# Cross stage: the first tile's first eight heads go to the DMA transpose as well, and all hinges and the gate come ahead of the third query's parts

## The reference

```python
x = x + _L0_attn_ref(_layernorm(x), ...)          # self attention over the batch axis, 16 heads of 32
x = x + _L0_xattn_ref(_layernorm(x), ctx, ctx, mask, ...)
x = x + _L0_ffn_ref(_layernorm(x), ...)

# cross attention
scores = jnp.einsum('bnlh,bnph->bnlp', qm, km) / np.sqrt(HEAD_DIM)
scores = jnp.where(mask, scores, MASK_FILL)
attn = jax.nn.softmax(scores, axis=-1)
out = jnp.einsum('bnlp,bnph->bnlh', attn, vm)
# ffn: 64 small functions of one variable, each a sum over 16 hinges
s = jnp.einsum('btd,dm->btm', x, Win) + bin_
h = jax.nn.relu(s[..., None] * W1 + b1)
g = jnp.einsum('btmh,mh->btm', h, W2) + b2
out = jnp.einsum('btm,md->btd', g, Wout) + bout
```

## Time and profile before

| | us |
|---|---|
| median of 3 runs | 1730.53 (1727.5 to 1731.91) |
| the profiled execution, its own time | 1728.16 |
| its span, first to last instruction | 1726.2 |
| TensorE busy | 1614.0 (93%) |
| VectorE busy | 1401.6 (81%) |
| GpSimd busy | 1172.5 (68%) |
| ScalarE busy | 975.0 (56%) |
| mean granted TensorE clock | 0.979 |

### The profile page before, as it was taken

One profiled execution on the slowest core, in us unless ns is written; L12 is line 12 of the kernel. 1 busy time (PEld: TensorE's weight loads), 2 busy tenths in 40 slices (PEclk: granted clock), 3 DMA queues, 4 the chain that ended last, 5 costly groups with the idle time before them and its releaser, 6 DMA issues.

```text
span 1726.2 us, 35517 instructions
## 1 busy us (share of the span) xinstructions
PE 1614.0 (93%) x13184; PEld 1326.2 (77%) x13184; DVE 1401.6 (81%) x1931; ACT 975.0 (56%) x2316; POOL 1172.5 (68%) x801
## 2 busy tenths in 40 slices
PE   6899999999999999999689999999999999999985
PEld 5678888888888888887577777777777777777774
DVE  6789888888898888877648888788888888888876
ACT  3434444433344444434348777777677787777773
POOL 3276666666677776669378667787667786677850
PEclk9999999999999999999789999999999999999997
DMA  5311111111111011144154444654455644365441
GB/s 215 124 34 47 50 50 49 49 49 49 30 43 49 24 49 49 49 92 76 50 106 77 98 96 113 125 103 111 87 113 113 131 95 106 94 111 123 100 81 55
DMA packets 241741, 140.89 MB, mean 82 GB/s; under 512 B 191168, under 2 KB 199488, under 8 KB 241600
## 3 DMA queue, kind: packets, MB, share of 16 engines
q1 hardware_dynamic: 241024, 138.92, 34.1%
q10 hardware_dynamic: 576, 0.07, 0.0%
HBM read 59.92 MB, written 37.09 MB: 56 GB/s over the span
## 4 chain that ended last, share of the span: by engine, by line
PE 67%; ACT 13%; DVE 9%; issue 6%; POOL 3%; DMA 2%; SPq 0%; ACTq 0%; POOLq 0%; DVEq 0%
PE qb L452 28%; PE ring L1548 12%; PE ob L588 10%; ACT prob_c L1761 7%; PE sc L1576 5%; PE ring L1553 4%; PE tb L460 3%; PE sc L1548 2%; DVE g_sb L1886 2%; PE sc L1568 2%; ACT pT L1727 2%; ACT sc L1740 1%; PE ring L1586 1%; ACT p L1777 1%; DMA w_first<-in_wqkv 1%
## 5 line engine op out<-in xcount | busy, mean ns | idle before, releaser
L452 PE MATMUL qb<-wqkv,xT 128*128 128x512 f32 x2304 | 552.1, 394 | 6.1 <-DVE wqkv L1022 6.1
L452 PEld LDWEIGHTS qb<-wqkv,xT 128*128 128x128 f32 x2304 | 429.8, 189 | 93.8 <-DVE wqkv L1022 6.3
L1761 ACT ACTIVATE prob_c<-sc,ntop 128x128 f32<-128x128 f32 x1024 | 284.2, 391 | 25.9 <-DVE ntop L1913 23.9
L1548 PE MATMUL ring<-wqkv 128*128 128x512 f32 x960 | 253.6, 409 | 28.5 <-DVE wqkv L1895 19.0
L1548 PEld LDWEIGHTS ring<-wqkv 128*128 128x128 f32 x960 | 174.5, 192 | 83.2 <-DVE wqkv L1895 25.5
L357 POOL TENSOR_TENSOR prod_pool<-v,prob 128x1024 f32<-128x1024 f32 x64 | 179.9, 2811 | 64.5 <-DVE prob L917 59.4
L1913 DVE TENSOR_REDUCE ntop<-sc 128x4 f32<-128x512 f32 x256 | 171.5, 681 | 26.5 <-PE sc L1576 26.5
L588 PE MATMUL ob<-wout,aT 128*128 128x512 f32 x768 | 191.5, 398 | 0.8 <-DVE aT L947 0.8
L668 ACT ACTIVATE v<-qb 128x512 f32<-128x512 f32 x64 | 38.3, 598 | 260.1 <-PE qb L452 249.7
L1479 POOL TENSOR_TENSOR p<-prob_c,p 128x1024 f16<-128x1024 f32 x80 | 171.6, 2145 | 16.3 <-ACT p L1777 16.2
L1548 PE MATMUL ring<-xT_c,wqkv 128*128 128x512 f32 x720 | 176.6, 401 | 2.6 <-DVE attn_c L1978 2.6
(11 more groups left out here) (153 smaller groups left out, 3267.5 us busy)
## 6 DMA issues: line engine op xcount, KB each, us to landing
x_tile<-in_x SPq DMA_DIRECT2D x16, 1024.0 KB, 5.5
x_scratch<-xres SPq DMA_DIRECT2D x16, 1024.0 KB, 4.6
x_tile<-x_scratch SPq DMA_DIRECT2D x16, 1024.0 KB, 5.5
out<-x SPq DMA_DIRECT2D x64, 256.0 KB, 2.0
kt<-k_scratch SPq DMA_DIRECT2D x16, 512.0 KB, 3.7
v_c<-v_scratch SPq DMA_DIRECT2D x16, 272.0 KB, 4.4
raw<-in_wqkv SPq DMA_DIRECT2D x3, 1024.0 KB, 8.9
pT<-p SPq DMA_TRANSPOSE x160, 3.2
```

The source lines that it names most:

```text
L452: last = nc.tensor.matmul(qb[g % 4][:, :], xT[p][a][:, k, t * P:(t + 1) * P], wqkv[b][:, k, c * D:(c + 1) * D], start=(n == 0), stop=(n == ...
L1548: last = nc.tensor.matmul(dst, s, m, start=(n == 0), stop=(n == len(terms) - 1))
L1761: last = nc.scalar.activation(prob[:, h, :], sc[g][:, (h % 4) * C:(h % 4 + 1) * C], ACT.Exp, bias=ntop[:, h:h + 1])
```

## The change

Four edits, all in the cross stage.

1. Heads 0 to 7 of tile 0 are turned by DMA: ScalarE writes their high part between the exponentials of heads 4 to 7 and those of heads 8 to 11 (`part_hi(0, 0)`), GpSimd the low part behind `norm(0)` and `norm(1)` (`part_lo(0, 0)`), SyncE issues `turn(j, 0, 0)` behind the first output store. Two `prob_T`, two `prob_hi` and two `prob_lo` a step go away.
2. The four quarters left (the last eight heads of tiles 0 and 1) are each done one tile later in the order: those of tile 0 in round t = 1, those of tile 1 in round t = 2, and `prob_hi` of the first of them stands ahead of `exps(t, 0)`.
3. `norm2_T(0)` goes ahead of `out_proj(0)` on TensorE, and the ring's turns follow.
4. The hinges are spread 4, 3, 1, 0 over the four queries in place of 3, 2, 2, 1, and the gate's parts stand ahead of the third query's parts, not the fourth's. On VectorE `normalise(3)` stands behind two hinges in place of three.

```diff
 def slot_turns(t):
     if t == 0:
-        return [("out", 0), ("aT", 0), ("pv", 0), ("wo", 0), ("x2T", 0), ("pT", 0), ("pT", 1)]
-    late = [("pT", 2 * t), ("pT", 2 * t + 1)]
+        return [("out", 0), ("aT", 0), ("pv", 0), ("x2T", 0), ("wo", 0)]
+    late = [("pT", 2 * t - 2), ("pT", 2 * t - 1)]
...
-HINGE_RUNS = ((0, 3), (3, 2), (5, 2), (7, 1))
+HINGE_RUNS = ((0, 4), (4, 3), (7, 1), (8, 0))
...
 def quarter(i):
-    return divmod(i if i < 4 else i + 2, 4)
+    return i // 2, i % 2 + 2

 def parts_over(j, t, part):
-    return (3 * j + t - 1, 2 * j + t - 2)[part]
+    return (4 * j + t, 2 * j + t - 2)[part]
...
                 for t in range(R - 1):                      # SyncE
                     if active(j, "out", t):
                         store(j, p, t)
-                    if t == 1 and has(j):
-                        turn(j, 1, 0)
+                    if t < 2 and has(j):
+                        turn(j, t, 0)
...
                     norm(0)                                 # GpSimd
                     norm(1)
+                part_lo(0, 0)
                 norm2(j, 1)
...
                 values(0)                                   # TensorE
+                norm2_T(0)
                 out_proj(0)
-                norm2_T(0)
-                prob_T(0)
-                prob_T(1)
                 for t in (1, 2):
                     scores(t)
                     attn_T(t)
-                    prob_T(2 * t)
-                    prob_T(2 * t + 1)
+                    prob_T(2 * t - 2)
+                    prob_T(2 * t - 1)
...
                     wait(act, topped, 16 * j + 4 * t + g + 1)     # exps(t, g) on ScalarE
-                    if t == 1 or (t == 2 and g >= 2):
-                        wait(act, psum["pT"], TURNS_OVER["pT"](j, g if t == 1 else g + 2))
+                    if t in (1, 2) and g >= 2:
+                        wait(act, psum["pT"], TURNS_OVER["pT"](j, 2 * t + g - 4))
                     else:
-                        wait(act, p_lo[g // 2], parts_over(j, max(t, 1 + g // 2), g // 2))
+                        wait(act, p_lo[g // 2], parts_over(j, max(t, 2 * (g // 2)), g // 2))
...
                 attn_hi(0)
-                for g in range(4):
-                    exps(0, g)
+                exps(0, 0)
+                exps(0, 1)
+                part_hi(0, 0)
+                exps(0, 2)
+                exps(0, 3)
                 for t in (1, 2):
                     norm2_hi(t - 1)
-                    if t == 1:
-                        prob_hi(0)
-                        prob_hi(1)
                     attn_hi(t)
+                    prob_hi(2 * t - 2)
                     exps(t, 0)
-                    prob_hi(2 * t)
-                    prob_hi(2 * t + 1)
+                    prob_hi(2 * t - 1)
                     exps(t, 1)
...
                 for m in range(DK):                         # VectorE
-                    hinges(*HINGE_RUNS[m])
                     if m == 0:
+                        hinges(0, 2)
                         normalise(3)
+                        hinges(2, 2)
                         norm2_lo(3)
-                    if m == 3:
+                    else:
+                        hinges(*HINGE_RUNS[m])
+                    if m == 2:
                         gate_lo()
```

More of the change, by code:

```diff
@@ L1200 @@
     "x2T": lambda j, i: 4 * j + i - 2,
-    "pT": lambda j, i: 6 * j + i + 1,
+    "pT": lambda j, i: 4 * j + i + 1,
     "xT": lambda j, i: 4 * j + i + 1,
@@ L1625, in values @@
                     if tile < 2:
-                        wait(pe, taken["pT"], TURNS_OVER["pT"](made, 2 * tile + 3))
+                        wait(pe, taken["pT"], TURNS_OVER["pT"](made, 2 * tile + 1))
                     if t == 1:
@@ L1632, in values @@
                         head = head_of(h)
-                        if h % 8 == 0 and tile > (0, 1)[h // 8]:
+                        if h % 8 == 0 and tile > (-1, 1)[h // 8]:
                             wait(pe, turned[h // 8], 32 * (parts_over(made, tile, h // 8) + 1))
@@ L1766, in prob_hi @@
                     t, g = quarter(i)
-                    if g == 0 or i == 4:
+                    if g == 2:
                         wait(act, psum["pv"], 4 * j + t - 1)
@@ L2021, in step @@
                     norm2_lo(t - 1)
-                    if t == 1:
-                        prob_lo(0)
                     tops(t, 0)
-                    if t == 1:
-                        prob_lo(1)
                     attn_lo(t)
                     tops(t, 1)
-                    prob_lo(2 * t)
+                    prob_lo(2 * t - 2)
                     add_out(t)
+                    prob_lo(2 * t - 1)
                     tops(t, 2)
-                    prob_lo(2 * t + 1)
                     tops(t, 3)
```

## The result

The changed kernel takes 1749.32 us (median of 4 runs, 1744.22 to 1752.88); the kernel before took 1729.01 beside it (4 runs, 1726.84 to 1731.91). The ratio is 1.0119, with a 95% interval of 1.0089 to 1.0148. The change makes the kernel slower by about 20 us. The profiled execution took 1751.09 us with a span of 1749.3, so 23.1 more span than before; its mean granted clock was 0.961 in place of 0.979. The two slower runs have the lower clocks, 0.961 and 0.962, the two faster ones (1744.22 and 1747.56) 0.968 and 0.966.

The account below looks back on a forecast made before the run. ScalarE's exponentials, not TensorE at 93% busy, were taken to set rounds 1 and 2. Steady steps with step 1 4.8, first step 7.6 and clock 7.6 sum to 20.0: 1750.5 on the median, stated as 1749, range 1739 to 1759.

Parts of the forecast that it names:

- Round 0: Steady steps, scores(0) to scores(1): ScalarE's copy, taken as 1.12 us, makes scores(1) start 0.63 us later.
- Gate and queries: End of a steady step: earlier gate gains 0.14 us, normalise(3) one hinge earlier 0.19, together 0.33 a step.
- The clock: TensorE idle 1.9 us ahead of scores(1) lowers its clock: 0.54 us a step, 14 times, 7.6 (bounds 0 and 26).
- The first step: Tile 1's exponentials wait for GpSimd's low part behind the norms and tokens: costs 7.6 us (bounds 6.4 and 10.7).
- The clock holds: Rival: steady cost and first step as forecast, no clock term, 12.4 us slower, 1743; chance 0.25.
- The first step hides its delay: Rival: GpSimd's order does not hold up ScalarE in the first step; 4.8 to 12.4 slower, 1735 to 1743; chance 0.08.
- TensorE's busy time is what counts: Rival: ScalarE's copy hides itself, so removed transposes win time; 13.7 us faster, 1717; strong form's chance 0.04.
- The mild form of the latter: Round 0's exponentials end as before, 1490.94; gain 0.49 + 0.33 a step, less 7.6 for the first step: 1727; chance 0.04.
- The signs I named: Profile after: waits of 1.8 to 2 us before scores(1), about 0.7 before scores(0); scores(0) to scores(1) 8.95; ScalarE some 11.

Follow-up runs that it names:

- the kernel with the unread matmuls: Changed kernel plus six 128x512 matmuls that nobody reads, on TensorE behind out_proj(0) and in front of scores(1): 1735.34 us, ratio 1.0040 to the kernel before.
- low part first: Changed kernel with GpSimd's low part of tile 0 ahead of norm(0), norm(1) and the token wait, in the first step alone: 1736.34 us, ratio 1.0043.
- copy behind with the first step mended: Changed kernel with ScalarE's copy behind all 16 exponentials and the first step's low part ahead of the tokens: 1723.59 us, ratio 0.9969 to the kernel before.

## Why the prediction was right, and where its terms were off

The forecast was 1749, and it came true by the mechanism it named: the copy between the exponentials makes TensorE wait in front of `scores(1)`, the first step waits for GpSimd behind the tokens, and the clock falls behind the new idle time. But two of the terms were off in size by about a factor of two or more, in opposite directions, so that the agreement to a third of a microsecond is luck: the span of the profiled execution grew by 23.1 and the median by 20.3, where the sum was 20.0 and the forecast lay 18.5 above the median of 1730.53 that it started from.

*Round 0.* The term held. I had 0.63, that is 8.18 to 8.81, and round 0 went to 8.78; the copy makes the exponentials 1.10 later, where I had taken 1.12, and moving it behind them gave back 1.08 (8.78 to 7.70). What was wrong is the sign that I named, 8.95. There I had let `scores(0)` start 0.14 earlier and left `scores(1)` where it was, though the whole chain from `scores(0)` to the last exponential moves with it. By the terms of the sum it should have read 8.81.

*Gate and queries.* Predicted gain 0.33 a step, measured 0.50, as the kernel with this edit alone shows too. I had counted 0.19 for the wait at the second query, and that was too little. Before, the 48 query matmuls of step 4 ran in two pieces:

```profile
1101.57 3.05 PE L1548 MATMUL ring<-xT_c,wqkv 128*128 128x512 f32 x12
1104.78 8.70 PE L1548 MATMUL ring<-xT_c,wqkv 128*128 128x512 f32 x36 [0.17 <-DVE attn_c L1978]
```

And now in one:

```profile
1111.12 11.48 PE L1549 MATMUL ring<-xT_c,wqkv 128*128 128x512 f32 x48
```

From the first start to the last end that is 11.91 and 11.48: 0.43 for a wait that shows 0.17. The other term, the gate, was predicted at 0.14 and gave the rest of the 0.50, some 0.06. Together the steady steps cost 0.10 each, 1.4 us in all, where I had 0.30 and 4.2: the term is the small difference of a loss (0.63, measured 0.60) and a gain (0.33, measured 0.50), and nearly all of the error is the gain's. Step 1, which I had counted with 0.6, cost nothing.

*The clock.* The term was 7.6 (14 times 0.54); it is 14.8, twice that. The nearest row, the start of step 1, was a fair guide to whether the clock falls and a poor one to what it costs: there the fall came late, and the scores ran mostly at the upper level (the transposes started 1.81 behind `scores(0)`, against 1.73 in step 11). In steps 12 to 15 of the changed kernel it comes just behind the start of the scores, they run at the lower level, and the step loses 2.2, more than the 1.86 that I had as the upper bound of a step. On the other hand it fell in 10 steps of 14 only, so that the sum lies inside the bounds of 0 and 26.

The Trainium skill, page "TensorE: Matmul & The Clock Gate", section "Why this matters for your kernels", reserves such drops for idle gaps longer than any of these. The traces do not agree: 1.83 to 1.88 us were enough in ten steps of 14, and with 0.47 to 0.51 it fell in none.

*The first step.* The group of exponentials that waits for GpSimd was to start at 868.65 and started at 868.90. `scores(2)` stood at 875.18, 0.7 later than predicted; 0.44 of this is a wait that I had not seen at all: the copy of tile 1 waits for the DMA transposes of tile 0, since it overwrites what they read. It was harmless here, and it became the main cost once the copy was moved behind. Near the end `values(3)` waited no longer, and the stretch from `scores(3)` to the next `scores(0)` took 24.39 in place of 27.16: 2.77 gained where I had guessed 1.5 between 0 and 2.66. On the other side `scores(3)` came 10.0 later than before, counted from the start of the stage, where I had 9.1. The sum was 7.6, measured 7.3: two errors of 0.9 and 1.3 that nearly cancel.

*The rivals.* "The clock holds" is answered by the kernel with the unread matmuls: it would have been 1735, not 1743. Steady steps and first step together cost 8.7 in the account of the changed kernel, not the 12.4 that I had, and in the profiled run with the unread matmuls the first two steps were another 1.3 shorter and the cross stage began 1.1 earlier. "The first step hides its delay" and "TensorE's busy time is what counts" are refuted by the rows of the first step and of step 11. The mild form of the latter, 1727 with the exponentials ending as before, is what the copy behind all exponentials gives in round 0 (7.70, with 8.18 - 0.49 = 7.69 forecast). But there the late transposes and the clock behind them took all of it back: steps 2 to 14 took 684.4 us in that profiled run and 683.4 before.

*The signs I named.* The waits stand where I said: 1.83 for `prob_c` ahead of `scores(1)`, the 0.81 for the gate and the 0.42 for `pT` gone, about 0.68 ahead of `scores(2)` and `scores(3)`, 9.86 where I had said some 11 on ScalarE in the first step. Off in size are the 8.95 (8.78) and the wait for `q_first`, 0.95 and not 0.7.

## What to carry to other kernels

When work is taken off an engine that a loop with another engine holds up, what is left is idle time; ask first whether the other engine gets longer (here by the copy, 1.1 us a step), and then what the idle time does to TensorE's clock, which here cost ten times what the steady step did. If the idle time can't be avoided, matmuls that nobody reads in front of the wait were free here, where TensorE would have waited anyway, and gave back 14 us. And of a change with several edits try each alone: here one edit of four was worth 8 us, and the other three cost 28.

## What the runs showed of the hardware that I had not expected

- The clock fell behind single idle times of 1.83 to 1.88 us in 10 steps of 14 and, with the same order of instructions in another kernel, in 8 of 14, in part others. Behind the 1.56 at the start of step 1 it fell in six kernels and held in three (low part first, unread matmuls, copy behind with the first step mended). It fell behind two idle times of about 1.0 to 1.2 and 1.28 close together (seven of seven such steps), behind a single one of 1.28 once in three, and never behind one of 0.75 alone. A fall cost between 0.6 and 2.3 us.
- With the copy behind, tile 0's DMA transposes (128x1024 fp16) held it up by 1.7 to 1.9 us in place of 0.2 in one to three steps of 14, not always the same ones, and by some 0.4 to 0.8 us in a few more. Moving the output store away did not change it, and what does is open.
- The 48 query matmuls, interrupted once for an idle time of 0.17 us, took 0.43 longer (11.91 in place of 11.48).
